# One fused residual kernel: W0 in four transfers, the adapters' product moved, eleven short products of zeros

## The reference, cut to what matters

```python
# layer 0: one adapter per sequence, 8 adapters of rank 16
H = jnp.einsum('btd,od->bto', x, W)                 # W is 512 x 512
xa = jnp.einsum('btd,brd->btr', x, A[adapter_idx])
delta = jnp.einsum('btr,bor->bto', xa, Bm[adapter_idx]) * scalings[adapter_idx][:, None, None]
x = x + H + delta
x = x + einsum('bct,bcd->bdt', x, w1[idx1])         # layer 1: one 64 x 64 matrix per sequence
x = x + attention(x, cond, Wq, Wk, Wv, Wo)          # layer 2: 16 heads, causal
x = x + einsum('bct,bcd->bdt', x, w3[idx3])         # layer 3: as layer 1
```

## Time and profile before

| what | value |
|---|---|
| median of 3 runs | 608.4 us (608.35 to 608.61) |
| the profiled execution's own time | 608.5 us |
| its span, first to last instruction | 606.8 us |
| TensorE matmuls (PE) busy | 599.6 us, 99% of the span, 8524 instructions |
| VectorE (DVE), ScalarE (ACT), GpSimd (POOL) busy | 392.5, 225.6, 110.2 us |
| DMA | 48.29 MB, mean 80 GB/s |

### The profile page before, as it was taken

The page is one execution under the profiler, slowest core; times in us unless marked ns, Lnnn a source line. Parts: engine busy times, 40 slices in busy tenths (PEclk is TensorE's granted clock), DMA queues, the critical chain, the costliest instruction groups (busy, mean ns, idle before and its releaser), DMA issues.

```text
span 606.8 us, 21505 instructions
## 1 busy us (share of the span) xinstructions
PE 599.6 (99%) x8524; PEld 519.4 (86%) x8524; DVE 392.5 (65%) x573; ACT 225.6 (37%) x434; POOL 110.2 (18%) x101
## 2 busy tenths in 40 slices
PE   8999999999999999999999999999999999999998
PEld 8898889798898988889798898978889898888885
DVE  4699865765657566564866657576564766647374
ACT  4555352343424244251443514244251433413222
POOL 2013120402104040130402104040130402103030
PEclk9999999999999999999999999999999999999999
DMA  9862322231412313222231413322222231310312
GB/s 294 167 137 64 87 57 77 75 70 66 96 40 86 86 61 74 72 65 73 74 82 55 96 39 89 84 68 67 72 67 71 76 89 47 71 67 3 70 42 105
DMA packets 65272, 48.29 MB, mean 80 GB/s; under 512 B 16922, under 2 KB 51738, under 8 KB 65242
## 3 DMA queue, kind: packets, MB, share of 16 engines
q1 hardware_dynamic: 60090, 42.63, 26.7%
q10 hardware_dynamic: 5152, 5.24, 3.1%
HBM read 30.54 MB, written 17.30 MB: 79 GB/s over the span
## 4 chain that ended last, share of the span: by engine, by line
PE 97%; DVE 1%; issue 1%; ACT 0%; DVEq 0%
PE banks L653 10%; PE banks L658 10%; PE banks L654 10%; PE banks L681 5%; PE banks L754 5%; PE banks L755 5%; PE banks L683 5%; PE banks L593 5%; PE banks L685 5%; PE banks L595 5%; PE banks L597 5%; PE banks L761 5%; PE banks L708 5%; PE banks L700 4%; PE banks L724 3%; PE banks L620 3%
## 5 line engine op out<-in xcount | busy, mean ns | idle before, releaser
L653 PE MATMUL banks<-x1T_hi,w_hi 128*128 128x256 f32 x512 | 130.0, 286 | 0.0
L654 PE MATMUL banks<-x1T_hi,w_lo 128*128 128x256 f32 x512 | 128.3, 283 | 0.0
L653 PEld LDWEIGHTS banks<-x1T_hi,w_hi 128*128 128x128 f32 x512 | 96.8, 189 | 0.7 <-ACT x1T_hi L926 0.4
L654 PEld LDWEIGHTS banks<-x1T_hi,w_lo 128*128 128x128 f32 x512 | 96.9, 189 | 0.0
L1429 POOL TENSOR_TENSOR w_own<-w_in,own 128x128 f32<-128x128 f32 x32 | 15.0, 471 | 382.0 <-PE banks L620 283.0
L658 PE MATMUL banks<-x1T_lo,w_hi 128*128 128x256 f32 x512 | 82.4, 283 | 0.0
L1447 POOL TENSOR_TENSOR probs<-probs,row_max 128x1024 f32<-128x1024 f32 x32 | 61.0, 1907 | 91.3 <-DVE row_max L1224 91.3
L658 PEld LDWEIGHTS banks<-x1T_lo,w_hi 128*128 128x128 f32 x512 | 70.2, 189 | 0.2
L926 ACT ACTIVATE attnT_hi<-banks 128x512 fp32r<-128x512 f32 (+1 forms) x32 | 17.1, 581 | 117.9 <-PE banks L724 117.5
L1210 DVE TENSOR_TENSOR qkT<-banks,beta 128x512 f32<-128x512 f32 x32 | 22.1, 691 | 59.3 <-PE banks L658 59.3
L1228 DVE TENSOR_REDUCE row_sum<-probs 128x16 f32<-128x1024 f32 x32 | 39.0, 1218 | 24.1 <-ACT probs L1008 24.1
(11 more groups left out here) (138 smaller groups left out, 1039.5 us busy)
## 6 DMA issues: line engine op xcount, KB each, us to landing
x_rows<-x_in SPq DMA_DIRECT2D x64, 128.0 KB, 2.4
x_kept<-x_rows SPq DMA_DIRECT2D x16, 512.0 KB, 3.6
x_in<-in_x_dram SPq DMA_DIRECT2D x60, 128.0 KB, 2.8
out_dram<-x_y SPq DMA_DIRECT2D x15, 512.0 KB, 2.8
b_sel<-b_parts SPq DMA_DIRECT2D x180, 32.0 KB, 1.7
w_in<-in_L_cond_weights_dram SPq DMA_DIRECT2D x128, 16.0 KB
probsT<-in_L_cond_W_dram ACTq DMA_DIRECT2D x1, 1024.0 KB, 6.4
probs<-in_L_cond_Wk_dram ACTq DMA_DIRECT2D x1, 1024.0 KB, 5.9
```

Source lines behind the costliest of these rows:

```text
L653: nc.tensor.matmul(out_ap, w_hi[:, w, c, cols], x1T_hi[:, c, :], start=(c == 0), stop=False)
L654: nc.tensor.matmul(out_ap, w_lo[:, w, c, cols], x1T_hi[:, c, :], start=False, stop=False)
```

## The change

W is loaded in four transfers of 128 rows, each with a semaphore of its own. The addition of the identity is now by row block: addition n adds a whole 128x128 identity to columns n*128 to n*128+127 of block n. The four additions are interleaved with the rests of x: two ahead of the first, one behind each. TensorE turns W0 by row block for the first three groups (three transposes after each addition), and the fourth group at the end. Layer 0's chunks take the high part's products of both tiles first and then those of the rest, with separate waits. `first_adapters_down` moves from behind chunk 0 to behind chunk 1. The products of zeros are eleven of 88 columns ahead of x's turn, and none behind it.

```diff
--- before.py
+++ after.py
@@ -164,7 +164,7 @@
 
 
         def diagonal(n):
-            return bass.AP(tensor=probsT, offset=n, ap=[[HG * HEADS * S, P], [D + P, NC], [NC, P // NC]])
+            return stage[W0][:, n, n * P:(n + 1) * P]
 
         banks = ctx.enter_context(nc.psum_tensor("banks", [P, 8 * BANK], F32))
         bank = [banks[:, b * BANK:(b + 1) * BANK] for b in range(8)]
@@ -186,6 +186,7 @@
         scal_loaded = sem("scal_loaded")
         b_ordered = sem("b_ordered")
         w_loaded = [sem(f"w_loaded{k}") for k in range(NW)]
+        w0_part_loaded = [sem(f"w0_part_loaded{n}") for n in range(NC)]
         x_first_loaded = sem("x_first_loaded")
         x_loaded = sem("x_loaded")
         b_parts_stored = sem("b_parts_stored")
@@ -524,16 +525,23 @@
 
             def turn_part(k, dc):
                 if dc == 0:
-                    if k != W0:
-                        pe.wait_ge(w_loaded[k], 16)
-                if k == W0:
-                    pe.wait_ge(diag_added, dc + 1)
+                    pe.wait_ge(w_loaded[k], 16)
                 turn(GROUPS_OF[k][dc], pieces_of(k, dc))
 
 
-            def stay_busy(n):
+            def turn_w0():
+                groups = GROUPS_OF[W0]
+                for oc in range(NC):
+                    pe.wait_ge(diag_added, oc + 1)
+                    for dc in range(NC - 1):
+                        turn_pieces(groups[dc], in_chunks(bank_of_group(groups[dc])), pieces_of(W0, dc), (oc,))
+                pe.wait_ge(first_copied, TILES)
+                turn_pieces(groups[-1], in_chunks(bank_of_group(groups[-1])), pieces_of(W0, NC - 1), range(NC))
+
+
+            def stay_busy(n, columns):
                 for _ in range(n):
-                    nc.tensor.matmul(bank[MIX[0]][:, 0:P], still[:], still[:], start=True, stop=True)
+                    nc.tensor.matmul(bank[MIX[0]][:, 0:columns], still[:], still[:, 0:columns], start=True, stop=True)
 
             def turn_first_x():
                 pe.wait_ge(x_first_loaded, 16)
@@ -596,6 +604,16 @@
                                  start=False, stop=False)
                 nc.tensor.matmul(bank[MIX[t]][:], xT_lo[:, c, tok(t)], w_hi[:, W0, c, :],
                                  start=False, stop=False)
+
+            def first_layer0_part(c):
+                pe.wait_ge(turned_hi, GROUPS_OF[W0][c] + 1)
+                for t in range(TILES):
+                    for x_part in (xT_hi, xT_lo):
+                        nc.tensor.matmul(bank[MIX[t]], x_part[:, c, tok(t)], w_hi[:, W0, c, :],
+                                         start=(c == 0 and x_part is xT_hi), stop=False)
+                pe.wait_ge(turned_lo, GROUPS_OF[W0][c] + 1)
+                for t in range(TILES):
+                    nc.tensor.matmul(bank[MIX[t]], xT_hi[:, c, tok(t)], w_lo[:, W0, c, :], start=False, stop=False)
 
             def layer0(i):
                 pe.wait_ge(xT_split, i)
@@ -855,27 +873,22 @@
                 attend_last()
 
             pe.wait_ge(still_set, 1)
-            stay_busy(8)
+            stay_busy(11, 88)
             pe.wait_ge(ident_step, 2)
             turn_first_x()
             pe.wait_ge(consts_step, 13)
             spread_rows()
-            stay_busy(3)
-            for c in range(NC):
-                if c == NC - 1:
-                    pe.wait_ge(first_copied, TILES)
-                turn_part(W0, c)
+            turn_w0()
             pe.wait_ge(a_loaded, 16)
             turn(GROUP_A, [every_fourth(a_nat, c) for c in range(NC)])
             for c in range(NC):
-                pe.wait_ge(turned_lo, GROUPS_OF[W0][c] + 1)
-                for t in range(TILES):
-                    layer0_part(t, c)
+                first_layer0_part(c)
                 if c == 0:
                     pe.wait_ge(b_ordered, 1)
                     turn(GROUP_B, [b_nat[:, n, :] for n in range(NC)], in_rows_of_b)
-                    first_adapters_down()
                 else:
+                    if c == 1:
+                        first_adapters_down()
                     turn_part(WK, c - 1)
             first_adapters_up()
             turn_part(WK, 3)
@@ -929,7 +942,8 @@
                 act.dma_start(stage[k], matrix.rearrange("(c p) d -> p c d", p=P)).then_inc(w_loaded[k], 16)
 
             act.dma_start(x_first, x_v[0]).then_inc(x_first_loaded, 16)
-            load_w(W0, W)
+            for n in range(NC):
+                act.dma_start(stage[W0][:, n, :], W[n * P:(n + 1) * P, :]).then_inc(w0_part_loaded[n], 16)
             act.dma_start(a_nat, A.rearrange("n r d -> (n r) d")).then_inc(a_loaded, 16)
             act.dma_start(b_in.rearrange("p (n e) -> p n e", n=ADAPTERS),
                           Bm.rearrange("n (p c) r -> p n (c r)", c=NC)).then_inc(b_in_loaded, 16)
@@ -1345,18 +1359,19 @@
             nc.vector.memset(still[:], 0.0).then_inc(still_set, 1)
             dve.wait_ge(idx0_loaded, 16)
             copy(idx0_first[:], idx0_row[:, 0:PSEQ]).then_inc(idx0_cast, 1)
+
+
+            def add_identity(n):
+                dve.wait_ge(w0_part_loaded[n], 16)
+                nc.vector.tensor_tensor(diagonal(n), diagonal(n), ident[:], ALU.add).then_inc(diag_added, 1)
+
+            dve.wait_ge(ident_step, 2)
+            for n in range(2):
+                add_identity(n)
             for t in range(TILES):
                 dve.wait_ge(first_hi_done, t + 1)
                 rest(xT_lo[:, :, tok(t)], in_chunks(bank[SC[t]]), xT_hi[:, :, tok(t)]).then_inc(first_lo_done, 1)
-
-
-            dve.wait_ge(ident_step, 2)
-            dve.wait_ge(w_loaded[W0], 16)
-            for n in range(NC):
-                columns = ident[:].rearrange("p (e c) -> p c e", c=NC)[:, n, :]
-                nc.vector.tensor_tensor(diagonal(n), diagonal(n),
-                                        columns.unsqueeze(1).to_broadcast([P, NC, P // NC]), ALU.add)\
-                    .then_inc(diag_added, 1)
+                add_identity(2 + t)
 
 
             dve.wait_ge(consts_step, 13)
```

## The result

The changed kernel takes 610.62 us in the median of 18 executions (608.84 to 612.87), the kernel before 608.50 of 18 (608.14 to 609.06). The ratio is 1.0026, with a 95% interval of 1.0017 to 1.0035: slower, clear of noise. The middle of the interval lies over the 0.2% that the prediction counts as a difference, its lower end a little under it. The forecast was 608.3, with 609.3 as its upper end.

A forecast was written before the change was run, and what follows sets the result against it. TensorE carries 97% of the chain that ended last, so only an earlier gapless start, in the first 10.6 us, counts. Layer 0 0.06 earlier and the moved product at zero sum to -0.06 on 608.4: 608.3, range 607.3 to 609.3.

The forecast's parts named there:

- Part 1's step of 0.213: Zero products ahead of x's turn: the 128-column weight load keeps each step at 0.213; x's high part 0.7 later.
- the stream's rival: Zero products: the stream sets the step, 0.147, so layer 0 starts at 9.76; -0.9, 607.5; chance 0.24.
- The step that failed: x's turn: clock still rises at 5.6, saving 0.2 on the zeros and putting all eight transposes at 0.12.
- The rival: Early stretch: clock rises later or falls; +0.6 for a rise at 9.0, +2.0 (610.4) reaching chunk 0; chance 0.11.
- Part 2: W0's load in four transfers: quarters land near 5.1, 5.9, 6.8 and 7.7; three extra issues cost 1.5, hidden.
- Parts 3 and 4: VectorE's and TensorE's order before layer 0: last W0 turn at 9.25, layer 0 at 10.58 for 10.64, 0.06 earlier.
- Part 5: Adapters' product moved behind chunk 1: the same 1.58, cost zero, bounded by 0 and 0.3.

The follow-up runs named there:

- run 5: The changed kernel with the zero products' weights cut to 88 columns as well as their streams; 607.59 us, ratio 0.9990 to the kernel before.
- run 1: The changed kernel with eight zero products of 128 columns again ahead of x's turn and none behind it; 611.14 us, ratio 1.0038.
- run 4: The changed kernel with both old stretches of zeros back, eight of 128 columns ahead of x's turn and three behind the spread rows; 608.33 us.
- run 6: The kernel of run 1 plus three products of zeros ahead of the second pair's first adapters' product; 608.39 us, ratio 0.9996.
- run 2: The changed kernel with its eleven zero products 128 columns wide instead of 88; 607.98 us, ratio 0.9992.
- run 3: The kernel before with eleven zero products of 88 columns for its first eight, the three behind x's turn kept; 611.70 us, ratio 1.0049.
- run 14: The kernel before with eleven 88-by-88 zero products for its first eight, the three of 128 columns behind x's turn kept; 608.51 us.
- run 7: The changed kernel with its eleven zero products 112 columns wide instead of 88; 608.33 us, ratio 0.9997.
- run 9: The kernel before with eleven 88-by-88 zero products in place of its eight and its three; 609.82 us, ratio 1.0023.
- run 12: The same kernel as run 9, run again for a profile of an execution with the clock's fall; 609.32 us.
- run 13: The same kernel as run 9, run once more for a profile with the clock's fall; 610.02 us.

## Why the prediction was wrong

**Part 1's step of 0.213: right.** It decided the case against the stream's rival, and run 5 shows the same by the other side. The Trainium skill's formula ("TensorE: Matmul & The Clock Gate", LDWEIGHTS), columns over 1.2 with no word on the clock, gives 107 ns for 128 columns. That fits the higher level here (0.11) and not the lower one, where the step is 0.213 for 88, 112 and 128 columns of stream.

**The step that failed** is in the paragraph behind it: "less 0.2 because the last two fall behind the rise at 5.6", and "All eight transposes are then at 0.12". I took the rise from the one profile of before and kept it where it was, while the change replaced the very products ahead of it. If the load of 128 columns sets the step and the stream is cut to 88, the streams no longer follow each other; I had both findings and did not put them together. The rise moved to 6.9 and 8.3 in two profiles of the lower cluster and to 13.5 and 15.2 in two of the upper one. In the first two, layer 0 starts at 10.86 and 11.22 (the lower cluster is +0.4 on the median); in the others at 13.40 (+2.5), where 10.58 was forecast. Even for products of 128 columns the 5.6 was an early case and no constant: behind the same eight products that the kernel before has, the clock rose at about 7.4, 7.2 and 6.9 in runs 1, 4 and 6.

**The rival was named and mis-weighed.** Its price, +0.6 for a rise at 9 and +2.0 once it reaches chunk 0, is near both clusters: +0.4, and +2.1 to +3.2. I gave it 0.11; ten of the eighteen executions are in its upper branch. It names the thinner streams, but rests its chance on the dropped products behind x's turn; runs 2 and 3 show the thinner streams ahead of it. The Trainium skill says that transposes do not count as TensorE's being busy in the same way (same page, Part 4, PE-mode transpose). What runs here show neither contradicts nor proves it: in the two profiles of the upper cluster the rise came after layer 0's first product (13.40; rises at 13.5 and 15.2), behind 7 us of transposes and spread rows, but in one of them only 0.07 after that product's start. In runs 3 and 14 the clock rose in the midst of W0's transposes, at 12.8 and 10.7, with products of zeros shortly before them, and run 6, with transposes alone from 7.5 to 9.9, kept its clock. So the rule alone is not enough to foretell a rise or a fall.

**Part 2: right but for a size.** Three more issues cost 0.48 each and the table load ended at 5.49. A, B and Wk came in time. The second quarter was forecast to land near 5.9; its addition began between 5.74 (runs 5 and 6) and 6.85 (run 7). In run 4 that put x's first rest off by 0.33, in none of these did TensorE lose by it.

**Parts 3 and 4: right in their mechanism.** In run 2, whose clock rises at 6.4, not far from the one assumed, layer 0 starts at 10.68 against 10.58 forecast, and 607.98 was measured against 608.3. That the time is lower by more than forecast is not the beginning's doing: in its profile layer 0 starts 0.04 later than before, the adapters' last products at 19.84 against 19.85, and the span is 0.3 shorter because two later waits of TensorE are 0.9 in all instead of 1.3. Why they differ is open. What parts 3 and 4 overlooked is the other use of the three products of zeros: in the new order they would no longer lie in a wait and would cost 0.77 (run 4), so dropping them is worth something there.

**Part 5: right.** In run 2 the moved product runs from 13.98 and the adapters' last products at 19.84, against 19.85 before. No gap opened in front of either.

**The range** was too narrow because I had one execution's clock as a fact. The three times shown of before agreed within 0.3, and that said nothing on how the new beginning would scatter.

## What to carry to other kernels

Products that only keep TensorE's clock up are part of the design, not filler: do not shorten their stream alone, since weights of 128 columns hold the step (0.213 here) while a shorter stream thins the work in it. Either keep the stream near the width of the weights (no late rise in 22 executions of runs 2 and 7) or shorten both (run 5; a late rise is then rare, not excluded). And ask of each whether it lies in a wait, where it is free, or on TensorE's path, where it costs its length (run 4). Where a change touches what stands ahead of a clock's rise, take the time of the rise from no profile of before, and look at several executions for clusters and for their mean clock. Transfers in parts pay (with the new order they start layer 0 1.1 us earlier, run 5 against run 9) only if the engine that waits for them has its clock.

## What the runs showed that I had not expected

The number of TensorE's instructions ahead of the loop matters. With 16 instructions of zeros (run 1) one profile has a wait of 1.49 in the midst of the second pair's scores, with half the clock behind it, and six of ten executions have a mean clock of 0.997 or less. With 22 in any place (the kernels before and after, runs 2, 4 to 13) or 28 (runs 3, 14) every profile has a single wait there, of 0.29 to 0.56 and with no fall behind it. Low means are then single ones, one execution of run 5, one of the changed kernel (612.87) and one of the kernel before (610.78), except in runs 9, 12 and 13, whose two profiled falls lie at 8 us. What in the layout does it was not tried. A second wait of TensorE, at 106 to 111 us, is 0.38 to 1.23 in all profiles whatever the kernel. That is of the size of the scatter within a cluster (0.4 in the lower, 1.1 in the upper one), but that it causes the scatter is not shown.
